# A two-layer MetaFormer kernel on one core: the second expert group's loop cut from two turns to one, row weights made four tiles at a time, sends in bursts of six

## The reference, cut to what matters

```python
x1 = x + L0_conv(...)            # gaussian pooling, 3x3 attention, 1x1 convolution, norm, leaky relu
# L0_ffn on the layer norm of x1: 8 experts, each token takes 2
top_logits, top_idx = top_k(x @ Wg, 2); top_w = softmax(top_logits)
act = silu(x @ W1[e]) * (x @ W3[e] + b3[e])      # 128 -> 384
out += weight * act @ W2[e]                      # 384 -> 128
x2 = x1 + out
x3 = x2 + L1_conv(layernorm(x2))                 # depthwise 7x7, weights from a codebook
# L1_ffn on the layer norm of x3: 8 experts of 512, 2 per token, with a capacity of 2560 rows each
```

## Time and profile before

| | |
|---|---|
| median of 3 runs | 2642.64 us |
| lowest and highest | 2631.65, 2645.08 us |
| the profiled execution's own time | 2620.37 us |
| its span in the profile | 2618.5 us |
| mean granted TensorE clock | 0.852 |
| PE, DVE, ACT, POOL busy | 69%, 46%, 31%, 38% |
| chain of work that ended last | PE 44%, issue 21%, DMA 12%, DVE 10%, ACT 4% |

### The profile page before, as it was taken

How to read it: one execution, slowest core, us unless ns; L and a number is a source line. 1 busy time by engine, 2 the same in 40 slices (tenths; PEclk the granted TensorE clock), 3 DMA queues, 4 the chain that set the end, 5 groups by cost and what they waited for, 6 DMA issues and landing times.

```text
span 2618.5 us, 40480 instructions
## 1 busy us (share of the span) xinstructions
PE 1806.9 (69%) x9815; PEld 1306.7 (50%) x9816; DVE 1216.0 (46%) x4690; ACT 812.9 (31%) x1759; POOL 986.6 (38%) x1009
## 2 busy tenths in 40 slices
PE   4999996992199998989878887089200003999963
PEld 4777775771055555555545554089200002666642
DVE  4466567645055555557656665825620000222238
ACT  1233232221144444445444544301100001444422
POOL 2000002434466665633222224400577773455430
PEclk8999998996599999999988999599655556999975
DMA  2215555567122222234343332354111000233248
GB/s 99 57 49 99 94 99 110 99 122 171 42 64 65 63 65 58 66 88 91 73 91 73 75 73 70 110 127 89 35 52 54 27 3 25 77 89 86 77 139 277
DMA packets 273226, 217.57 MB, mean 83 GB/s; under 512 B 65377, under 2 KB 249462, under 8 KB 272842
## 3 DMA queue, kind: packets, MB, share of 16 engines
q1 hardware_dynamic: 208842, 148.18, 25.4%
q0 software_dynamic: 30464, 55.93, 6.6%
q10 hardware_dynamic: 33792, 12.06, 1.7%
HBM read 110.11 MB, written 105.14 MB: 82 GB/s over the span
## 4 chain that ended last, share of the span: by engine, by line
PE 44%; issue 21%; DMA 12%; DVE 10%; ACT 4%; another core or an unknown queue 3%; DVEq 2%; POOL 1%; SPq 1%; POOLq 0%; ACTq 0%
DMA slots<-arena 7%; PE tp L854 6%; PE zp L981 5%; PE zp L690 5%; PE tp L870 4%; PE tp L879 4%; PE zp L845 3%; PE tp L994 3%; PE gp L840 3%; DMA out<-arena 2%; PE tp L772 1%; PE gp L787 1%; DMA arena<-taps 1%; DVE arena L1697 1%
## 5 line engine op out<-in xcount | busy, mean ns | idle before, releaser
L586 POOL DMA_INDIRECT slots<-arena x256 | 251.8, 984 | 597.8 <-DVE arena L1474 409.6
L605 POOL DMA_INDIRECT results<-arena x272 | 264.6, 973 | 488.9 <-DVE arena L1533 358.7
L1545 DVE TENSOR_TENSOR arena<-tp,arena 128x384 f32<-128x384 f32 x272 | 151.7, 558 | 440.6 <-PE tp L879 336.7
L586 POOL DMA_INDIRECT slots_cap<-arena x256 | 253.6, 990 | 227.8 <-DVE arena L1499 150.1
L690 PE MATMUL zp<-arena 128*128 128x256 f32 x1024 | 239.9, 388 | 29.9 <-ACT arena L1035 29.4
L854 PE MATMUL tp<-arena 128*128 x1632 | 255.7, 294 | 0.4
L870 PE MATMUL tp<-arena 128*128 x544 | 233.5, 512 | 5.7 <-issue 1.2
L653 POOL DMA_INDIRECT results<-arena x160 | 158.1, 988 | 183.4 <-DVE arena L1712 144.6
L879 PE MATMUL tp<-arena 128*128 x544 | 226.9, 500 | 0.0
L690 PEld LDWEIGHTS zp<-arena 128*128 128x128 f32 x1024 | 195.4, 194 | 59.3 <-ACT arena L1035 31.4
L974 PE MATMUL gp<-arena 128*128 128x128 f32 x160 | 27.1, 293 | 284.3 <-issue 277.6
(11 more groups left out here) (256 smaller groups left out, 3167.6 us busy)
## 6 DMA issues: line engine op xcount, KB each, us to landing
arena<-results SPq DMA_DIRECT2D x48, 512.0 KB, 5.5
slots<-arena SPq DMA_DIRECT2D x8, 2278.0 KB, 19.2
arena<-slots SPq DMA_DIRECT2D x272, 67.0 KB
arena<-taps SPq DMA_DIRECT2D x64, 224.0 KB, 4.2
slots_cap<-arena SPq DMA_DIRECT2D x16, 670.0 KB
arena<-slots_cap SPq DMA_DIRECT2D x40, 268.0 KB
arena<-in_x SPq DMA_DIRECT2D x8, 1024.0 KB, 7.7
arena<-arena SPq DMA_DIRECT2D x128, 64.0 KB
```

Source lines behind the costliest of these rows:

```text
L586: g.indirect_dma_start(slots[m], bass.IndirectOffsetOnAxis(ap=slot[:, k, blk:blk + 1].bitcast(U32), axis=0), rows[:, blk, :], None, bounds ...
L605: g.indirect_dma_start(results, bass.IndirectOffsetOnAxis(ap=row_at[:, q:q + 1].bitcast(U32), axis=0), y_tile[q], None, bounds_check=2 * T ...
```

## The change

1. `send` of group 0: POOL waits after every third block for its last six sends (it was every second and the last four).
2. On ACT `tok_n_out` of T + 2 moves from behind `hidden_out` to directly behind `tok_t_out`, in both groups.
3. `flag` and `row_weight` become `flags`: at tiles 0 and 4 of a turn one comparison over the columns of four tiles, at tiles 1 and 5 a product, the row numbers and a sum over four columns. `w_own` then rises by four. The eight tile buffers become one array.
4. Group 1: one buffer of loaded results in place of two, a column of mean and deviation for each of the 128 blocks in place of two sets of eight, and a loop of one turn on SP, ACT and DVE, with one turn written out ahead of it. SP's load of the results of a turn now waits for the sum of the turn before (`x2_ready` of `turn`, it was `turn - 1`), and the tile loads of the turn stand behind that wait. DVE no longer waits for ACT's normalising before it writes means and deviations.

```diff
-                if n % 2:
-                    for j in range(SENDS_AHEAD // 2):
+                if n % BURST == BURST - 1:
+                    for j in range(2 * BURST):
                         last = 2 * n + 1 - j
                         pool.wait_ge(sem(f"sent{last % SENDS_AHEAD}"), 16 * (last // SENDS_AHEAD + 1))
...
-            def beside(turn, u):
-
+            def beside(turn):
+
+                if not isinstance(turn, int):
+                    sp.wait_ge(sem("x2_ready"), turn)
+                    load_results([y_in], "y_in0", turn, 0)
+                load_tiles(1, turn)
                 if isinstance(turn, int):
-                    for q in range(RING if turn == 0 else 0):
-                        sp.wait_ge(sem(f"y_out{q}"), 16 * turns)
-                else:
-                    sp.wait_ge(sem("x2_ready"), turn - 1)
-                if not (isinstance(turn, int) and turn == 0):
-                    load_results(y_in, f"y_in{u}", turn, u)
-                load_tiles(1, turn)
-                if isinstance(turn, int) and turn == 0:
-                    load_results(y_in, f"y_in{u}", turn, u)
+                    load_results([y_in], "y_in0", turn, 0)
                 fill_slots(2, rows * turn, rows)
 
-            for u in range(2):
-                beside(u, u)
-            with sp.Fori(1, turns // 2) as turn:
-                for u in range(2):
-                    beside(2 * turn + u, u)
+            for q in range(RING):
+                sp.wait_ge(sem(f"y_out{q}"), 16 * turns)
+            beside(0)
+            with sp.Fori(1, turns - 1) as turn:
+                beside(turn)
             load_tiles(1, turns - 1)
...
                     if not (last and q == RING - 1):
                         tok_t_out(T + 1, 1 - u)
+                    if not (last and q >= RING - 2):
+                        tok_n_out(g, turn + (q + 2) // RING, (q + 2) % RING)
                     if not (first and q == 0):
                         act_t_out(T - 1, 1 - u)
                     hidden_out(T, u)
-                    if not (last and q >= RING - 2):
-                        tok_n_out(g, turn + (q + 2) // RING, (q + 2) % RING)
...
+            def flags(g, turn, q):
+
+                N, h = 2 * (g * turns + turn), q // FLAGS
+                part = slice(FLAGS * h, FLAGS * h + FLAGS)
+                if q % FLAGS == 0:
+                    for k in range(q, q + FLAGS):
+                        dve.wait_ge(sem(f"tile_in{k}"), 16 * (g * turns + turn + 1))
+                    v.tensor_tensor(second[:, part], tiles_in[:, part, SLOT0], own[:, bass.ds(RING * turn + q, FLAGS)], ALU.not_equal
+                                    ).then_inc(sem("flagged"), 1)
+                elif q % FLAGS == 1:
+                    dve.wait_ge(sem("flagged"), N + h + 1)
+                    v.tensor_tensor(y_w[:, part], tiles_in[:, part, DW], second[:, part], ALU.mult).then_inc(sem("w_step"), 1)
+                    v.tensor_tensor(row_no[:, part], tiles_in[:, part, ID], second[:, part], ALU.add)
+                    dve.wait_ge(sem("w_step"), N + h + 1)
+                    v.tensor_tensor(y_w[:, part], y_w[:, part], tiles_in[:, part, W0], ALU.add).then_inc(sem("w_own"), FLAGS)
...
-            turn_tiles(1, 0, True, False, beside=(0, 0, 0))
-            turn_tiles(1, 1, False, False, beside=(1, 1, 0))
-            with dve.Fori(1, turns // 2) as turn:
-                for u in range(2):
-                    turn_tiles(1, 2 * turn + u, False, False, beside=(2 * turn + u, u, turn))
+            turn_tiles(1, 0, True, False, beside=0)
+            with dve.Fori(1, turns - 1) as turn:
+                turn_tiles(1, turn, False, False, beside=turn)
             turn_tiles(1, turns - 1, False, True)
```

More of the change, by code:

```diff
@@ L229, in metaformer @@
         m3_s = arena.take(E8 * F0)
-        tile_in = [arena.take(ROW_W) for _ in range(RING)]
+        tiles_in = arena.take(RING, ROW_W)
+        tile_in = [tiles_in[:, q, :] for q in range(RING)]
         act_t = [arena.take(FC0, P) for _ in range(2)]
@@ L244, in metaformer @@
         row_at = arena.take(RING)
-        mean_2, rstd_2 = arena.take(2 * KB), arena.take(2 * KB)
-        mean_c, rstd_c = ([z[:, KB * u:KB * (u + 1)] for u in range(2)] for z in (mean_2, rstd_2))
+        mean_2, rstd_2 = arena.take(NBLK), arena.take(NBLK)
         var_c = arena.take(2 * KB)
@@ L259, in metaformer @@
         arena.at = routing
-        y_in = [arena.take(KB // 2, 2, P) for _ in range(2)]
+        y_in = arena.take(KB // 2, 2, P)
         arena.at = phase
@@ L1180, in _ @@
             turn_tiles(1, 0, True, False)
[L1181 to L1185, removed]
+            with act.Fori(1, turns - 1) as turn:
+                turn_tiles(1, turn, False, False, beside=turn - 1)
+            turn_tiles(1, turns - 1, False, True, beside=turns - 2)
             def normalise_two(turn):
@@ L1190, in normalise_two @@
                     for k in range(KB):
-                        normalise(2 * turn + u, u, k, blocks=KB, before=KB)
+                        normalise(2 * turn + u, k, blocks=KB, before=KB)
             with act.Fori(KB // 2, KB) as turn:
@@ L1511, in _ @@
             turns = TILES0 // RING
[L1513 to L1522, removed]
-                v.tensor_tensor(row_no[:, q:q + 1], tile_in[q][:, ID:ID + 1], second[:, q:q + 1], ALU.add)
-                v.scalar_tensor_tensor(out=y_w[:, q:q + 1], in0=tile_in[q][:, DW:DW + 1], scalar=second[:, q:q + 1],
-                                       in1=tile_in[q][:, W0:W0 + 1], op0=ALU.mult, op1=ALU.add).then_inc(sem("w_own"), 1)
+            def flags(g, turn, q):
[12 more added lines that the diff above has]
+                    v.tensor_tensor(y_w[:, part], y_w[:, part], tiles_in[:, part, W0], ALU.add).then_inc(sem("w_own"), FLAGS)
             def y_out_of(g, turn, q):
@@ L1550, in turn_tiles @@
                     v.tensor_tensor(act_h[u], act_h[u], act_g[u], ALU.mult).then_inc(sem("act_ready"), 1)
-                    row_weight(T, q)
+                    flags(g, turn, q)
                     if not (first and q < 2):
@@ L1582, in scales, with chunk_sum @@
                     o.end()
-            def chunk_sum(n, u, turn, part):
-                o, blocks = sums[u], KC
-                mean, rstd = mean_c[u][:, 0:blocks], rstd_c[u][:, 0:blocks]
+            def chunk_sum(n, part):
+                o, blocks = sums[0], KC
+                mean, rstd = (z[:, bass.ds(blocks * n, blocks)] for z in (mean_2, rstd_2))
                 if part == 0:
-                    o = sums[u] = Order(dve, sem("dve_sum"), n, SUM_LINKS)
-                    dve.wait_ge(sem(f"y_in{u}"), 16 * (turn + 1))
-                    o.step(add_expert(n, u, 0, y_in))
+                    o = sums[0] = Order(dve, sem("dve_sum"), n, SUM_LINKS)
+                    dve.wait_ge(sem("y_in0"), 16 * (n + 1))
+                    o.step(add_expert(n, 0, y_in))
                 elif part == 1:
                     o.settle()
-                    add_expert(n, u, 1, y_in).then_inc(sem("x2_ready"), 1)
+                    add_expert(n, 1, y_in).then_inc(sem("x2_ready"), 1)
                 elif part == 2:
@@ L1632, in _ @@
                 o.link(last)
-                dve.wait_ge(sem("xn3_ready"), KB + 2 * turn)
-                token_stats(v, o, st_c, mean_2, var_c, rst_c, 1e-6, 2 * KB)
-                scales(o, mean_2, rstd_2, 2 * KB, True, True, 2)
+                mean, rstd = (z[:, bass.ds(2 * KB * turn, 2 * KB)] for z in (mean_2, rstd_2))
+                token_stats(v, o, st_c, mean, var_c, rst_c, 1e-6, 2 * KB)
+                scales(o, mean, rstd, 2 * KB, True, True, 2)
             dve.wait_ge(sem("biased"), NBLK // KB)
```

31 lines of the change are left out of this document (15 added, 16 removed).

## The result

| | before | changed |
|---|---|---|
| median | 2639.77 us (2631.65 to 2645.08, 4 runs) | 2609.28 us (2604.82 to 2612.76, 4 runs) |
| the profiled execution's own time, span | 2620.37, 2618.5 us | 2612.76, 2611.0 us |
| ratio, 95% interval | | 0.988 [0.984, 0.992] |

The change is faster by 1.2%, 30 us, where 122 us were forecast; 2609 us lies above the range of 2470 to 2580 us. The two profiled executions differ by 7.6 us only, because that of before stood 19 us under its median and that of the change 3.5 us above.

The account below looks back on a forecast made before the run. It took POOL to bound group 0's sends, a ring of PE and ACT the quiet tiles, and DVE's pauses group 1's later turns; -20 - 36 - 49.5 - 23 + 6 = -122 us from 2642.6 gave 2520 us, range 2470 to 2580 us.

Parts of the forecast that it names:

- ACT's order, group 0: Group 0's tiles: with normalising second on ACT the next transpose no longer waits for it; 0.30 us per tile, -36 us.
- Rival B: Group 0 keeps its pace, since something other than ACT's order sets 3.085 us per tile; 2557 us, chance 0.25.
- the ring of PE and ACT: Quiet tiles of group 1: PE's next transpose waits for ACT's normalising, losing 0.21 us of 2.80 us per tile.
- Bursts: Sends of group 0: bursts of six need 21 waits in place of 32, at 1.83 us each; -20 us.
- Group 1: Group 1's turns: DVE's loop of one turn -49.5 us, tiles -23 us, one buffer of results +6 us.
- The pause: DVE idle 7.34 us at each branch back of group 1's two-turn loop; with PE's clock 8.25 us each, six 49.5 us.
- rival D: Group 1: each of 14 branches back refetches instructions at 8.25 us, 115.5 us in place of 49.5 us; chance 0.06.
- Tiles of group 1: Five tiles per turn gain 0.21 us each, tiles 6 and 7 gain 0.25 us each; 15 turns, -23 us.
- One buffer of results: Group 1: tile loads behind the results may come late and hold ACT in tile 6; 0.4 us x 15, +6 us.
- rival C: Group 1: tile loads late every turn stall ACT, DVE and PE, +27 to +45 us; 2550 us, chance 0.12.

Follow-up runs that it names:

- e4: The kernel before with only ACT's new order (`tok_n_out` directly behind `tok_t_out`); 2669.9 us against 2642.2 us for before, ratio 1.010.
- f4: The kernel before with only `flags` (row weights made in fours); 2677.4 us against 2654.0 us for before, ratio 1.012.
- e2: The changed kernel with `flag` and `row_weight` restored, tile by tile; 2621.3 us against 2642.2 us for before, ratio 0.993.
- h1: The changed kernel run again, unaltered, on a quiet chip; 2458.5 us against 2563.1 us for before, ratio 0.959.
- f3: The changed kernel with a 448-column memset and a wait on POOL ahead of each send beside group 0; 2589.0 us against 2654.0 us for before, ratio 0.979.

## Why the prediction was wrong, and where it was right

- **ACT's order, group 0: -36 us forecast, the step that failed.** The prediction saw ACT's copy 1.75 us late and reckoned "if that lateness stays"; its least favourable end was "nothing gained". On a late chip the lateness belongs to PE's signals beside two indirect DMAs per tile, and is no constant: the profiled pair lost 62 us in group 0 (some 40 us, if the 19 us by which before's profiled execution was under its median lie there). `flags`, put at nothing in group 0, does the same by itself. By medians, less what each gained in group 1, e4 lost 28 + 13 = 41 us and f4 23 + 22 = 45 us there. Rival B had the right suspicion and too mild a price. On quiet chips a tile went from 2.81 to 2.62 us (22.5 and 21.0 us per turn), 24 us in 16 turns, order and flags together, so the ring of PE and ACT was read right in the main.
- **Bursts: -20 forecast, -25 measured.** The burst of 9.49 us is exact; the rest came from disturbed waits.
- **Group 1: -49.5 - 23 + 6 = -66.5 us forecast, -53 measured; the shares were wrong.** The pause went: 14 branches back cost 0.23 us each, and rival D is refuted. But the price, pairs of 58.25 us less two quiet turns of 25.0 us, took for granted that a turn of the new loop costs what a quiet turn did. By the table of group 1 the short loop with its buffer is worth 28 or 20 us, not 43.5. Part of it comes back in each turn: with the old flags its turns take 25.0 and 26.4 us, where e4's quiet turn takes 24.3; with the new flags 25.6 us, where f4's takes 25.2. The order gave 12 to 13 us, where 16 were forecast, the flags 12 to 22, where 7.5 were.

  What a long body costs shows in f4, where the flags shorten the two-turn body from 379 to 349 instructions: its pairs take 54.7 us, and DVE's idle time at the branch is 3.95 us against 7.34 us:

```profile
1388.73 0.56 DVE L1549 TENSOR_TENSOR arena<-tp,arena 128x384 f32<-128x384 f32 x1 [3.95 <-issue]
```

  Bodies of 127, 177 and 193 (e2) instructions never paused. More fetches don't explain the difference between the two long ones: both have 20 instruction packets in four passes. Whether the length itself decides, or where the body lies in the instruction memory, was not separated.

  The Trainium skill's page "Runtime: NRT & Kernel Launch", section "Instruction fetch mechanics", has a branch stall when its target is outside a window of two pages, 512 instructions in all on most engines. These runs neither bear it out nor refute it: 349 and 379 instructions are fewer than that, but can lie across three pages, and where a page begins no run shows. Its reading in the prediction, by which a short loop too could stall at every branch, did not come true.
- **Tiles of group 1, within that.** Three tiles, not five, were of the 2.80 us kind and gained 0.24 each. Tile 5 lost 0.19 us to the four-column work, and tile 6, put at a gain of 0.25, lost 0.34 (tile 7 gained nothing), because the register loads of DVE and PE came to overlap ahead of tile 7, which no row of before shows.
- **One buffer of results: +6 forecast.** ACT waits for a tile load once a turn, 11.1 us in 13 waits, 1.0 us the longest, as foreseen; rival C did not come.
- **Sum.** -25 + 62 - 53 + 9 = -7 us for the profiled pair, -30 us in the medians, since before's profiled execution was a lucky one. On quiet chips -104.6 us, where -122 us had been forecast. There h1 and h4 (before, with a memset that costs nothing) split it on one chip: sends -27, group 0 -26, group 1 -54, all else +2 us.

What stays open is why PE's signals come late on these chips. All that was shown is that it takes two indirect DMAs per tile on POOL, and that 1.31 us without one after each pair ends it. Which edit is best hangs on the chip: the change as it is where the signals are on time (f3's gap was not run there; the smaller one cost 66 us), f3's gap where they are late (2589 against 2605 to 2609 us, on different chips).

## What to carry to other kernels

A wait in which a consumer starts long after its producer ended is not a fixed cost: find what delays it before you speed up the work around it, and give the term an end on the losing side. Time before and after on more than one chip: one edit was worth 1.2% on one and 4.1% on another. On DVE each branch back cost microseconds with bodies of 349 and 379 instructions and nothing to speak of with 193 or fewer; shortening such a body can be worth more than what the removed instructions took (the same flags gave 22 us in the long loop, 12 us in the short one). And price a new loop by its own turns, not by the best turns of the old one.

## What the runs showed of the hardware that was not expected

- The same kernel took 2637 to 2654 us on three chips and 2562 us on two others. In group 0 PE's signals came up to 4 us late on the first three only, and only beside two indirect DMAs per tile without a gap of 1.31 us.
- Register loads of DVE and PE that overlap take 0.93 and 0.92 us in place of 0.31.
- Behind a memset with a wait on POOL the next indirect DMA starts 0.82 us later; behind one without a wait, 0.19 us.
- A branch back on DVE: 0.23 us for a body of 177 instructions; with a body of 349 DVE stood idle 3.95 us around it, with 379 7.34 us.
